# Adapter weights split in pieces inside the cms loop, adapter down products ahead of LayerNorm, sqrt and scaling row by row, and the cms sum added to the residual on VectorE

## The reference

```python
# layer 0, for each of B = 4 sequences, V = 512, H = 2048
attn = softmax((x @ Wq) @ (x @ Wk).T * V ** -0.5)
attn_out = (attn @ (x @ Wv)) @ Wp + bp
cms = gelu(attn_out @ cW1 + cb1) @ cW2 + cb2 + one_hot(code)
mod = gelu(concat([attn_out, cms]) @ mW1 + mb1) @ mW2 + mb2
y = clip(x + cms + mod, 0, 1)
# layer 1: one of E = 3 experts per sequence, 512 -> 256 -> 512
h = gelu(y @ W_down[e] + b_down[e]) @ W_up[e] + b_up[e]
h = y + h
out = (h - mean(h)) * rsqrt(var(h) + 1e-5) * ln_w[e] + ln_b[e]
```

## Time and profile before

| | us |
|---|---|
| median of 3 runs | 1168.14 |
| the profiled execution | 1168.62 |
| its span, first to last instruction | 1166.8 |
| TensorE busy | 1135.2 |
| DVE, ACT, POOL busy | 609.4, 348.2, 190.8 |
| TensorE's mean granted clock | 0.991 of full speed |

### The profile page before, as it was taken

One profiled execution on the slowest core, in us unless ns is written; L12 is line 12 of the kernel. 1 busy time (PEld: TensorE's weight loads), 2 busy tenths in 40 slices (PEclk: granted clock), 3 DMA queues, 4 the chain that ended last, 5 costly groups with the idle time before them and its releaser, 6 DMA issues.

```text
span 1166.8 us, 13772 instructions
## 1 busy us (share of the span) xinstructions
PE 1135.2 (97%) x5024; PEld 937.9 (80%) x5024; DVE 609.4 (52%) x907; ACT 348.2 (30%) x602; POOL 190.8 (16%) x132
## 2 busy tenths in 40 slices
PE   7997999999999999999899999999999999999995
PEld 6885888788888888888788888888888888888884
DVE  3735344265665665665874444434444454444775
ACT  3633333322322322223422121211212122121654
POOL 0523201110010110110731110101111110101014
PEclk9998999999999999999999999999999999999998
DMA  7332130001001001001000000000000000002622
GB/s 253 130 123 80 65 108 19 19 19 37 18 18 36 18 18 36 18 20 44 28 28 28 21 7 27 27 27 27 27 27 27 27 1 26 27 28 79 245 75 108
DMA packets 45617, 58.15 MB, mean 50 GB/s; under 512 B 3601, under 2 KB 29713, under 8 KB 43793
## 3 DMA queue, kind: packets, MB, share of 16 engines
q1 hardware_dynamic: 45008, 56.67, 14.3%
q10 hardware_dynamic: 576, 1.05, 0.2%
HBM read 47.22 MB, written 10.49 MB: 49 GB/s over the span
## 4 chain that ended last, share of the span: by engine, by line
PE 91%; DVE 4%; ACT 2%; issue 1%; POOL 1%; DMA 0%; DVEq 0%; ACTq 0%
PE bank L443 30%; PE bank L444 30%; PE bank L445 30%; DVE stats L965 1%; POOL res L416 1%; DVE wsplit L958 1%; PE bank L487 0%; DVE attn_lo L913 0%; ACT z_even L772 0%; DVE z_odd L973 0%; DVE z_even L973 0%; POOL wsplit L385 0%; DMA WqT_raw<-WqT_dram 0%; ACT attn_hi L611 0%; DVE mean_var L967 0%
## 5 line engine op out<-in xcount | busy, mean ns | idle before, releaser
L895 DVE TENSOR_TENSOR res<-bank,res 128x512 f32<-128x512 f32 x240 | 163.9, 692 | 262.7 <-PE bank L445 262.7
L703 ACT ACTIVATE gelu_f<-bank,hidden_bias 128x512 f32<-128x512 f32 x128 | 88.3, 690 | 637.7 <-PE bank L445 637.6
L895 DVE TENSOR_TENSOR cms_acc<-bank,cms_acc 128x512 f32<-128x512 f32 x240 | 163.4, 691 | 121.7 <-PE bank L445 121.7
L385 POOL TENSOR_TENSOR wsplit<-raw,wsplit 128x512 fp32r<-128x512 f32 (+1 forms) x64 | 101.0, 1580 | 721.5 <-ACT wsplit L620 721.5
L443 PE MATMUL bank<-attn_hi,wsplit 128*128 128x512 f32 x512 | 200.1, 391 | 3.1 <-DVE cms_lo L902 3.1
L443 PE MATMUL bank<-gelu_hi,wsplit 128*128 128x512 f32 x512 | 199.3, 389 | 0.8 <-DVE gelu_lo L881 0.8
L444 PE MATMUL bank<-attn_lo,wsplit 128*128 128x512 f32 x512 | 199.8, 390 | 0.0
L445 PE MATMUL bank<-attn_hi,wsplit 128*128 128x512 f32 x512 | 199.7, 390 | 0.0
L444 PE MATMUL bank<-gelu_lo,wsplit 128*128 128x512 f32 x512 | 199.2, 389 | 0.0
L445 PE MATMUL bank<-gelu_hi,wsplit 128*128 128x512 f32 x512 | 199.2, 389 | 0.0
L443 PEld LDWEIGHTS bank<-attn_hi,wsplit 128*128 128x128 f32 x512 | 96.5, 189 | 23.7 <-DVE cms_lo L902 3.5
(11 more groups left out here) (118 smaller groups left out, 1193.9 us busy)
## 6 DMA issues: line engine op xcount, KB each, us to landing
raw<-cW_dram SPq DMA_DIRECT2D x32, 256.0 KB, 2.8
raw<-mW_dram SPq DMA_DIRECT2D x16, 512.0 KB, 4.2
res<-xT_dram SPq DMA_DIRECT2D x4, 1024.0 KB, 8.2
x_raw<-x_dram SPq DMA_DIRECT2D x4, 1024.0 KB, 6.7
raw<-mW_dram SPq DMA_DIRECT2D x16, 256.0 KB, 4.4
cms_hi<-experts_split SPq DMA_DIRECT2D x4, 1024.0 KB, 4.8
cms_lo<-experts_split SPq DMA_DIRECT2D x4, 1024.0 KB, 6.8
experts_split<-attn_hi SPq DMA_DIRECT2D x3, 1024.0 KB, 8.3
```

What stands on the lines that cost most here:

```text
L385: pool.tensor_tensor(dst, src, f32(hi), ALU.subtract).then_inc(done, 1)
L703: act.activation(dst[:, g, :], bank[r][:, :], ACT.Gelu, bias=hidden_bias[:, s:s + 1]).then_inc(gelu_made, 1)
L895: op = dve.tensor_tensor(dst, src, dst, ALU.add)
```

## The change

The weights of the adapters arrive as one array `adapter` of 3 experts by 4 parts by 128 x 512 (laid out on the host), and are split in 12 such pieces, one in each of the cms blocks 2 to 13: ACT writes the hi part in the unit of sequence 0, POOL the lo part behind the block's weights, SP stores both and loads the next piece. The pieces use parts of `raw` and `wsplit` that are free in the cms stage. Nothing of the adapters is left in the attention stage.

The sum of `cms_acc` into `res` moves from POOL into DVE's `cms_final`, and TensorE waits for `cms_lo` only between the attn half and the cms half of the hidden product in the first four mod units.

In the last stage TensorE runs down(2) ahead of up(0) and down(3) ahead of up(1). Every row block of every sequence goes its own way through sqrt, reciprocal and scaling; each sequence has its own `z`; ACT's order is gelu(0), y, gelu(1), gelu(2), two `add_b_up`, norm of sequence 0, gelu(3), all other norms. POOL adds ln_b for 15 row blocks, DVE for the last one.

```diff
-        ROWS_ON_POOL = 2
-        SPLIT_AFTER = [(0, TT - 1), (1, 1), (1, TT - 1)]
+        POOL_ROWS = TT * B - 1
...
+        def splits_done(n):
+            return 2 * n + min(max(n - 2, 0), PIECES)
+        piece_raw = raw[:, 512:1024]
+        def piece(s):
+            return wsplit[:, s, 0:512], wsplit[:, s, 512:1024]
...
             load_cms(0)
-            with sp.Fori(1, NBLK) as n:
-                sp.wait_ge(w_split, n * 2)
+            for n in range(1, NBLK):
+                sp.wait_ge(w_split, splits_done(n - 1) + 2)
                 load_cms(n)
+                p = n - 2
+                if 0 < p <= PIECES:
+                    sp.wait_ge(w_split, splits_done(n))
+                    save_piece(p - 1)
+                if p > 1:
+                    sp.wait_ge(piece_saved, 32 * (p - 1))
+                if 0 <= p < PIECES:
+                    load_piece(p)
...
-                    if (b, t) in SPLIT_AFTER:
-                        e = SPLIT_AFTER.index((b, t))
-                        for half in (slice(0, 1024), slice(1024, 2048)):
-                            pool.wait_ge(expert_hi_made, 2 * e + 1 + (half.start > 0))
-                            lo(expert_lo[:, half], expert_raw[:, half], expert_hi[:, half], expert_lo_made)
...
-            def add_cms(r):
-                for m in range(KT):
-                    pool.wait_ge(summed, 4 * (CMS_UNITS - B + r) + m + 1)
-                    pool.tensor_tensor(res[:, r, m, :], res[:, r, m, :], cms_acc[:, r, m, :], ALU.add).then_inc(res_added, 1)
+            def split_piece(p):
+                pool.wait_ge(piece_hi_made, p + 1)
+                hi, low = piece(p % 2)
+                lo(low, piece_raw, hi, w_split)
+            for n in range(NBLK):
+                split_block(n, n % 2, False)
+                if 0 <= n - 2 < PIECES:
+                    split_piece(n - 2)
...
+                if isinstance(i, int) and CMS_UNITS <= i < CMS_UNITS + B:
+                    product(bank[r][:, :], terms[:KT], last_one=False)
+                    pe.wait_ge(cms_lo_made, KT * (r + 1))
+                    product(bank[r][:, :], terms[KT:], first_one=False).then_inc(h_filled, 1)
...
             adapter_down(1)
+            adapter_down(2)
             adapter_up(0)
-            adapter_down(2)
+            adapter_down(3)
             adapter_up(1)
-            adapter_down(3)
             adapter_up(2)
             adapter_up(3)
...
+                if r == 0 and not mod and not isinstance(n, int):
+                    act.wait_ge(piece_loaded, (n - 1) * 16)
+                    act.activation(piece(s)[0], piece_raw, ACT.Copy).then_inc(piece_hi_made, 1)
...
+            def norm(n):
+                b, t = n // TT, n % TT
+                act.wait_ge(var_made, n + 1)
+                act.activation(std[:, t:t + 1], mean_var[:, t, 1:2], ACT.Sqrt, bias=eps[:, :]).then_inc(std_made, 1)
+                if n < POOL_ROWS:
+                    act.wait_ge(rstd_made, n + 1)
+                    act.activation(z[b][:, t, :], z[b][:, t, :], ACT.Copy, scale=rstd[:, t:t + 1]).then_inc(normed, 1)
...
             def cms_final(r):
                 for m in range(KT):
+                    dve.tensor_tensor(res[:, r, m, :], res[:, r, m, :], cms_acc[:, r, m, :], ALU.add)
                     dve.wait_ge(cms_hi_made, KT * r + m + 1)
-                    dve.wait_ge(res_added, KT * r + m + 1)
...
-                if b < B - 1:
-                    dve.wait_ge(std_made, TT * (b + 1))
-                    dve.reciprocal(rstd[:, :], std[:, :]).then_inc(rstd_made, 1)
+                    dve.wait_ge(std_made, n + 1)
+                    dve.reciprocal(rstd[:, t:t + 1], std[:, t:t + 1]).then_inc(rstd_made, 1)
```

More of the change, by code:

```diff
@@ L18, in layers_kernel @@
     HID = cW1.shape[1]
[L19 to L20 removed]
+    BN = b_down_cols.shape[2] * P
+    E = b_down_cols.shape[0]
     KT = V // P
@@ L127, in layers_kernel @@
         raw_loaded = sem("raw_loaded")
[L128 to L131, removed]
+        piece_loaded = sem("piece_loaded")
+        piece_hi_made = sem("piece_hi_made")
+        piece_saved = sem("piece_saved")
         adapter_loaded = [sem(f"adapter_loaded{b}") for b in range(B)]
         rows_loaded = [sem(f"rows_loaded{b}") for b in range(B)]
-        stored = [[sem(f"stored_{k}_{t}") for t in range(TT)] for k in range(2)]
+        stored = sem("stored")
         const_made = sem("const_made")
@@ L182, in layers_kernel @@
         normed = sem("normed")
-        z_done = [sem(f"z_done{t}") for t in range(TT)]
+        z_done = sem("z_done")
         order = []
@@ L291, in _ @@
             load_xT(3)
[L293 to L308, removed]
+            for b in range(1, B):
                 sp.wait_ge(x_split, TT * b)
                 load_x(b)
[L312 to L319, removed]
             def load_cms(n):
@@ L353, in store @@
                 for t in range(TT):
[L354 to L368 removed]
+                    if TT * b + t < POOL_ROWS:
+                        sp.wait_ge(z_done, TT * b + t + 1)
+                    else:
+                        sp.wait_ge(last_done, TT * b + t - POOL_ROWS + 1)
+                    sp.dma_start(out[b, t * P:(t + 1) * P, :], z[b][:, t, :]).then_inc(stored, 16)
+            for b in range(B):
+                load_adapter(b)
+                if b == 0:
+                    load_rows(0)
+            for b in range(1, B):
+                load_rows(b)
+            for b in range(B):
                 store(b)
[L370 to L372 removed]
+            sp.wait_ge(stored, 16 * TT * B)
         @block.gpsimd
@@ L763, in gelu_adapter @@
                     act.activation(g1(b, 0)[:, m, :], bank[i % 4][:, :], ACT.Gelu, bias=bias[:, c:c + 1]).then_inc(gelu_made, 1)
-            def norm(b):
-                rows = slice(0, TT)
-                act.wait_ge(var_made, TT * (b + 1))
-                act.activation(std[:, rows], mean_var[:, rows, 1:2].rearrange("p t a -> p (t a)"), ACT.Sqrt, bias=eps[:, :]).then_inc(std_made, TT)
-                act.wait_ge(rstd_made, b + 1)
-                for t in range(TT):
-                    act.wait_ge(centred, TT * b + t + 1)
-                    act.activation(z[b % 2][:, t, :], z[b % 2][:, t, :], ACT.Copy, scale=rstd[:, t:t + 1]).then_inc(normed, 1)
@@ L782, in _ @@
             gelu_adapter(0)
             y_final(B - 1)
+            gelu_adapter(1)
+            gelu_adapter(2)
             add_b_up(B - 2)
-            gelu_adapter(1)
             add_b_up(B - 1)
-            norm(0)
-            gelu_adapter(2)
-            norm(1)
+            for t in range(TT):
+                norm(t)
             gelu_adapter(3)
-            norm(2)
-            last_norm(3)
+            for n in range(TT, TT * B):
+                norm(n)
         @block.vector
@@ L991, in _ @@
             y_final(B - 1)
-            for b in range(B):
-                if b < B - 1:
-                    gelu_lo_adapter(b + 1)
-                layer_norm(b)
+            gelu_lo_adapter(1)
+            gelu_lo_adapter(2)
+            layer_norm(0)
+            layer_norm(1)
+            gelu_lo_adapter(3)
+            layer_norm(2)
+            layer_norm(3)
 def kernel(**inputs):
@@ L1014 @@
                 "b_down_cols": columns(own["b_down"]), "b_up_cols": columns(own["b_up"])}
-    for name in ("Wp", "cW1", "cW2", "mW1", "mW2", "W_down", "W_up", "ln_w", "ln_b"):
+    E, V, BN = own["W_down"].shape
+    down = own["W_down"].reshape(E, V // P, P, BN).swapaxes(1, 2).reshape(E, P, 2, V).swapaxes(1, 2)
+    laid_out["adapter"] = _np.concatenate([down, own["W_up"].reshape(E, BN // P, P, V)], axis=1)
+    for name in ("Wp", "cW1", "cW2", "mW1", "mW2", "ln_w", "ln_b"):
         laid_out[name] = own[name]
```

123 lines of the change are left out of this document (45 added, 78 removed).

## The result

The changed kernel took 1147.82 us (median of 4 runs, 1146.93 to 1148.30) against 1168.12 us before: a ratio of 0.9825, with an interval of [0.9808, 0.9842]. The prediction was 1149.2 us. The profiled execution took 1147.69 us with a span of 1145.9, so the two traces differ by 1166.8 - 1145.9 = 20.9 us, and 18.9 were predicted.

The account below looks back on a forecast made before the run. TensorE, working almost without a gap, was taken as the bound; 10.7 (A) + 0 (pieces) + 3.0 (B) + 5.2 (C) = 18.9 us off 1168.62 gave 1149.7, so 1149.2 for the median; range 1145.8 to 1154.8.

Parts of the forecast that it names:

- A: Attention stage: without the expert splits, TensorE's 7.8 us wait and 2.9 us of slow clock go, 10.7 us gained.
- next late is the split of PT on DVE: Attention stage: this split ends at 99.95, before TensorE would come to the A tile at 100.49, so the whole wait goes.
- Pieces: Cms stage: 12 splits, each adding 0.6 us to ACT and 1.3 us to POOL per block, cost 0.
- upper bound of 0.25 us in each block: Cms stage: the most the pieces might cost, 0.25 us in each of 12 blocks, 3 us in all.
- Rival 4: Cms stage: a store and load chain over 21.8 us would stop TensorE in 11 blocks, 1202 us; chance 0.03.
- B: Start of mod stage: later cms_lo wait and additions on DVE gain 3.1 + 1.7 - 1.8 = 3.0 us; bounds 4.8 and 0.
- 1.8 us of small TensorE waits: Mod stage start: loss assumed from POOL's weight splits holding up DVE, none near the 3.1 us that lowers the clock.
- 2.9 us of waits: Mod stage start: TensorE's waits if POOL and two-SBUF-input DVE instructions exclude each other whole, leaving a gain of 1.9 us.
- Rival 1: Mod stage start: DVE's lag crosses TensorE by over about 3 us, clock falls, no gain, 1152.2 us; chance 0.13.
- Rival 3: Mod and last stages: B's waits all vanish and C overlaps better, 1.8 and 1.3 us more, 1146.1 us; chance 0.12.
- C: Last stage: the new order removes three round trips through ACT's tables, 5.2 us gained; bounds 1.5 and 6.5.
- gelu_lo(3): Last stage: DVE's split for sequence 3, taken as 1.8 us in the final chain, ending at 1144.57.

Follow-up runs that it names:

- a_only: Kernel before with only the adapter weights split in 12 pieces in the cms blocks, none in the attention stage: 1157.75 us (ratio 0.991).
- b_only: Kernel before with only cms added to the residual by DVE in cms_final and TensorE's later wait for cms_lo: 1163.06 us (ratio 0.9955).
- c_only: Kernel before with only the new order of the last stage, row by row sqrt and scaling: 1163.39 us (ratio 0.9963).
- pool_adds: Changed kernel with the additions of cms to the residual put back on POOL, TensorE's wait staying in the middle of the units: 1152.1 us (ratio 0.9866).
- pieces_twice: Changed kernel with POOL's subtraction of each of the 12 pieces made twice: 1148.22 us (ratio 0.983).
- pieces_wide: Changed kernel with an unused 128 x 1536 POOL subtraction ahead of each piece's split, which then waits for gelu_lo: 1160.3 us (ratio 0.9938).
- wait_early: Changed kernel with TensorE's wait for cms_lo put back ahead of each of the first four mod units: 1148.26 us (ratio 0.9838).

## Why the prediction was right

**What bounds the kernel.** TensorE did, in all but the named places: the 443 matmuls per 100 us did not move.

**A, 10.7 predicted, 10.9 found** (10.1 by `a_only`, with the slow part behind the wait as uncertain as said above). The step "next late is the split of PT on DVE" held too: it ended at 99.17, before TensorE came.

**Pieces, 0 predicted.** Found in the trace and bounded by experiment. The argument was half right. That the piece ends before `gelu_lo` starts is in the trace (412.69 + 1.30 = 413.99 against 414.07), but it isn't what makes the piece free: a second split of the same size, which doesn't end before, costs nothing either. The upper bound of 0.25 us in each block was of the right kind: a longer instruction ahead of `gelu_lo` does cost time, but first it uses up 1.0 us of slack. Rival 4, the chain of transfers, had no support: the stores landed in 2.8 us, in this row of DMA issues (count, KB of one, median us to landing).

```profile
experts_split<-wsplit SPq DMA_DIRECT2D x24, 256.0 KB, 2.8
```

**B, 3.0 predicted, 4.8 found** (4.8 by `b_only`). The mis-sized term is "1.8 us of small TensorE waits". The trace has about 0.2 us, from the one `gelu_lo` at 550.07, which was called for ("up to 0.35"). The rest assumed that the splits of block 17 hold DVE up by 0 to 3.7 us, from a row in which POOL meets a subtraction of two SBUF operands. For all but their first moment they met additions from a bank, which POOL did not hold up (0.75 to 0.76 us each, with a split beside them or without). The Trainium skill ("SBUF — State Buffer", on the shared port pair) restricts the exclusion to VectorE instructions with two SBUF inputs; I quoted that and then did not ask which of DVE's instructions would be under way at 576. The 2.9 us of waits that the prediction put down to this rule don't follow from it, since nearly all of DVE's time beside these splits has a bank as a source. `cms_final` took 4.9 us and the unit 7.8 to 8.0, a little less than the 5.0 and 8.2 worked out. Rival 1, a falling clock, did not appear. Rival 3 (1146.1) had B right, with no waits left.

**C, 5.2 predicted, 4.4 found** (4.4 by `c_only`). The stands were predicted at 4.3 and 3 us and were 4.13 and 2.74; rows were predicted at 1.73 and took 1.67. The mis-sized term is `gelu_lo(3)`: 1.8 us by the earlier trace rows, 2.78 in fact. The row that I took the price from met only the end of POOL's additions, 0.65 us of this one of before; after the change it meets two whole ones.

```profile
1140.19 5.03 POOL L435 TENSOR_TENSOR z_odd<-z_odd,ln_rows 128x512 f32<-128x512 f32 x4 [10.02 <-ACT z_odd L772]
```

TensorE's one new stop, 1.4 us for `z`, is the one that the prediction had in letting up(3) start only behind row 0 of sequence 2. It was harmless, as there: up(3) started at 1130.67, so its first row was in the bank near 1132.5, and DVE took it at 1135.52. C was tested as a whole; what the new order of TensorE's products and the square root row by row each bring was not measured apart.

**The sum.** 18.9 against 20.9 us: +0.2 in A, +1.8 in B, -0.8 in C, and 0.8 that lies in the start of the program. B's and C's errors partly cancelled, which was luck; the mechanisms of A, B and C were right.

## What to carry to other kernels

Before an operation of one engine is charged for another engine's work beside it, look at which instruction of the other will be under way at that time, and at where its operands lie. On the same two engines one meeting cost 1.25 us, another cost nothing, and a third cost POOL instead of DVE. A delay has to be set against the slack of the thing that it delays: 12 pieces of 1.3 us were free, and so were 24 of them, while the same 12 places with an instruction of 3.5 us cost 12.3 us. Where a stage ends in a chain over two engines, list what each does while it stands for the other; two calls moved into such stands gave 4.3 to 4.6 us more.

## What the runs showed of the hardware

- POOL and DVE excluded each other for whole instructions where both read two SBUF operands. Where POOL was first by 0.5 us or more, DVE waited for its end (0.5 us in `pool_adds`, 557.17 against 557.69; 1.0 us at 549.03 and 550.07 in the changed kernel); where DVE was first, or the two began within 0.02 us of each other, POOL waited. An addition on DVE with a bank as one source was not held up (0.75 to 0.76 us). A 128 x 512 subtraction on DVE took 0.68 us alone, 1.93 behind a POOL split of 2.42 us, and 2.68 behind one of 3.51 us; in `pieces_twice` it kept its 0.68, and POOL's two splits took 3.21 us instead of 2.6.
- The granted clock fell behind some stops of TensorE and not behind others. It was low (0.57) behind the 3.12 us of the earlier trace rows, which `a_only` repeated with 0.70 and `c_only` with 0.50 (573 to 579 us), and behind a stop of 2.45 us for `z_even` in the last stage of the kernel before (0.66 from 1147 to 1152). It stayed at 1.00 behind the 1.4 us for `z` in the changed kernel (1127 to 1134). It stayed at 1.00 in `pool_adds` with four stops of 0.18 to 1.06 us within 23 us, and in the 100 us of `pieces_wide` with a stop of about 0.77 us in every 23. How many matmuls run at the slow pitch behind one and the same stop differed between executions (14, 12 and 10 behind 7.81 us, 8 and 14 behind 3.12).
- The first matmuls of the program run at the pitch of 0.43 us, and how many do differs from one execution to the next: 6 in `wait_early`, 9 in the changed kernel, 13 in the kernel before and in `pieces_twice`, with the same first instructions. By that the first gelu's table load moved from 216.02 to 217.49 us between `wait_early` and `pieces_twice`.

```profile
216.02 1.28 ACT L677 ACT_TABLE_LOAD   x1 [1.98 <-PE bank L431]
```

```profile
217.49 1.28 ACT L683 ACT_TABLE_LOAD   x1 [1.99 <-PE bank L434]
```
